# A gated memory over chunks: two steps of VectorE and ten of sixteen scatters change their place in the turn

## The reference, cut to what matters

```python
def step(carry, inp):                       # _L0_attn_ref, over 3137 tokens, 16 images
    M, n, m = carry
    qt, kt, vt, li, lf, op = inp
    m_next = jnp.maximum(lf + m, li)
    i_s = jnp.exp(li - m_next)
    f_s = jnp.exp(lf + m - m_next)
    M = f_s[:, :, None] * M + i_s[:, :, None] * (vt[:, :, None] * kt[:, None, :])
    n = f_s * n + i_s * kt
    h_raw = jnp.einsum('bij,bj->bi', M, qt)
    denom = jnp.maximum(jnp.abs(jnp.einsum('bi,bi->b', n, qt))[:, None], 1e-06)
    h = jax.nn.sigmoid(op) * (h_raw / denom)
    return ((M, n, m_next), h)
...
h = h + _L0_attn_ref(_layernorm(h, axis=-1), ...)        # rms norm of the output inside
h = h + _L0_ffn_ref(_layernorm(h, axis=-1), ...)
# _L0_ffn_ref: logits = x @ gate_w + gate_b; idx = argmax; pos = cumsum of the one-hot;
#              buf[idx, pos] = x; two layers by expert; gather back
```

## Time and profile before

| | us |
|---|---|
| median of 3 runs (3207.86 to 3208.52) | 3207.94 |
| the profiled execution | 3205.61 |
| its span from first to last instruction | 3203.7 |

### The profile page before, as it was taken

One profiled execution on the slowest core, in us unless ns is written; L12 is line 12 of the kernel. 1 busy time (PEld: TensorE's weight loads), 2 busy tenths in 40 slices (PEclk: granted clock), 3 DMA queues, 4 the chain that ended last, 5 costly groups with the idle time before them and its releaser, 6 DMA issues. The chain is left out here.

```text
span 3203.7 us, 68709 instructions
## 1 busy us (share of the span) xinstructions
PE 2828.8 (88%) x25818; PEld 1557.7 (49%) x25818; DVE 2414.1 (75%) x3224; ACT 2182.1 (68%) x3138; POOL 1916.0 (60%) x1191
## 2 busy tenths in 40 slices
PE   7999999969999999995599958899999999999997
PEld 5666666635555555553244413344444444444444
DVE  6888888858888888884387637777777777777783
ACT  6777777758887888872244447677777777777762
POOL 8888888811677777777200066666666666666530
PEclk9999999989999999996799969999999999999999
DMA  1111111111221221211444421111212211212111
GB/s 48 42 42 39 42 40 42 39 59 37 61 72 54 73 60 51 62 43 51 145 149 151 137 61 35 36 54 46 58 52 52 56 52 53 56 49 55 47 35 49
DMA packets 208269, 191.21 MB, mean 60 GB/s; under 512 B 76381, under 2 KB 163398, under 8 KB 207562
## 3 DMA queue, kind: packets, MB, share of 16 engines
q1 hardware_dynamic: 173850, 142.95, 15.4%
q0 software_dynamic: 25600, 26.01, 3.3%
q10 hardware_dynamic: 8496, 17.87, 1.5%
HBM read 99.08 MB, written 87.65 MB: 58 GB/s over the span
## 5 line engine op out<-in xcount | busy, mean ns | idle before, releaser
L2428 POOL TENSOR_TENSOR E_w<-E_w,E_rs 128x1024 f32<-128x1024 f32 x200 | 408.9, 2044 | 406.5 <-DVE E_rs L2336 406.5
L2421 POOL DMA_INDIRECT E_row<-yb,P_gi x400 | 388.4, 971 | 395.4 <-POOLq L93 301.6
L689 POOL DMA_INDIRECT xb<-B_yt,P_gi x400 | 469.0, 1172 | 115.4 <-issue 113.9
L204 POOL TENSOR_TENSOR A_kmask<-A_ksb,A_pack_a 128x3584 f32<-128x3584 f32 x56 | 356.2, 6361 | 115.3 <-ACT A_ksb L374 115.3
L2220 ACT ACTIVATE E_w<-E_w 128x1024 f32<-128x1024 f32 x200 | 211.6, 1058 | 241.0 <-DVE E_w L2329 241.0
L2333 DVE TENSOR_REDUCE E_sm<-E_w 128x16 f32<-128x1024 f32 x200 | 243.8, 1219 | 127.0 <-ACT E_w L2220 125.2
L2321 DVE TENSOR_REDUCE E_mx<-E_lg 128x16 f32<-128x1024 f32 x200 | 242.1, 1210 | 114.8 <-PE E_lg L1985 113.9
L474 DVE COPY A_vbd<-A_v 128x512 f32<-128x512 f32 x336 | 215.6, 684 | 74.3 <-PE A_v L324 74.3
L2329 DVE TENSOR_TENSOR E_w<-E_lg,E_mx 128x1024 f32<-128x1024 f32 x200 | 244.7, 1223 | 6.4
L2016 PEld LDWEIGHTS E_wt<-S_pack_f,E_w 128*128 128x128 f32 (+1 forms) x1600 | 169.6, 141 | 159.1 <-issue 132.6
L1985 PE MATMUL E_lg<-S_wxs,E_yo 64*128 64x512 f32 x800 | 228.0, 646 | 7.6 <-DVE E_w L2329 7.4
(11 more groups left out here) (321 smaller groups left out, 6803.3 us busy)
## 6 DMA issues: line engine op xcount, KB each, us to landing
R_xs<-xb SPq DMA_DIRECT2D x57, 256.0 KB, 2.7
yb<-R_ys SPq DMA_DIRECT2D x57, 256.0 KB, 2.0
B_x<-h SPq DMA_DIRECT2D x25, 512.0 KB, 4.0
h<-B_hh SPq DMA_DIRECT2D x25, 512.0 KB, 3.2
A_xg<-in_xw SPq DMA_DIRECT2D x56, 224.0 KB, 2.5
h<-A_res ACTq DMA_DIRECT2D x56, 224.0 KB, 2.5
E_hx<-h SPq DMA_DIRECT2D x48, 256.0 KB, 2.6
out<-E_ob SPq DMA_DIRECT2D x96, 128.0 KB
```

The lines of the kernel that those rows point to most:

```text
L204: nc.gpsimd.tensor_tensor(kmask[i % 2][:], bc(ksb[i % 2][:].unsqueeze(2), [128, J, H, Q]), bc(head_of_row[:].unsqueeze(1).unsqueeze(3), [1 ...
L689: pool.indirect_dma_start(out=xb, out_offset=bass.IndirectOffsetOnAxis(ap=routed.gi[0:k, c, b:b + 1], axis=0), in_=yt[c % LT][0:k, D * row ...
L2421: pool.indirect_dma_start(out=row[b % LR][:, k, i], out_offset=None, in_=yb, in_offset=bass.IndirectOffsetOnAxis(ap=idx[:, c, 2 * n + i:2 ...
L2428: TT(w3, w3, bc(rs[g % 3][:].unsqueeze(2), [128, 2 * SH, G]), ALU.mult).then_inc(w_done, 1)
```

## The change

No operation is added or taken away. On DVE `outputs` goes from the head of the turn (for chunk t-2) to the end of the turn before (chunk t-1), between `forget_middle` and `forget_sum`; `slots` and `numbers` go ahead of `norm_sum`; `norm_query` and `normed_out` go ahead of `forget_middle`. On POOL the first ten images of a chunk are scattered at the end of turn t = chunk + 4, and the other six in the turn after, between `weigh_keys` and `age_memory`; before, all sixteen went in turn chunk + 5, five of them at that place and eleven at the end.

```diff
                 for t in range(CHUNKS + 5):
                     at(weigh_keys, t - 1)
-                    at(scatter, t - 5, range(0, 5))
+                    at(scatter, t - 5, range(10, B))
                     at(age_memory, t - 2)
                     at(scale_memory, t - 1)
-                    at(scatter, t - 5, range(5, B))
+                    at(scatter, t - 4, range(0, 10))
...
                 for t in range(CHUNKS + 4):
-                    at(outputs, t - 2)
                     at(ends, t - 1)
                     at(exponents, t - 1)
                     at(first_max, t - 1)
...
                     at(ranked, t - 4)
                     at(first_norm, t - 1)
                     at(own, t - 4)
+                    at(slots, t - 4)
+                    at(numbers, t - 4)
                     at(norm_sum, t - 1)
-                    at(slots, t - 4)
                     at(gate_out, t - 1)
-                    at(numbers, t - 4)
                     at(norm_weight, t - 1)
+                    at(norm_query, t - 1)
+                    at(normed_out, t - 2)
                     at(forget_middle, t)
-                    at(norm_query, t - 1)
+                    at(outputs, t - 1)
                     at(forget_sum, t)
                     at(last_max, t - 1)
                     at(last_norm, t - 1)
-                    at(normed_out, t - 2)
```

## The result

The changed kernel takes 3271.45 us (median of 4 runs, 3263.53 to 3273.82), before 3207.9: 1.0188 times as long, 95% interval 1.0176 to 1.0201. The forecast of 3209 and its range to 3245 both missed. It went the way of rival D, and beyond D's 3244.

A forecast was written before the change was run, and what follows sets the result against it. PE and DVE's ring bound the turn, POOL second; after the change POOL sets it. First turns -1.4, twenty turns +12.4, end -12.7 and +3.0 give +1.3 us: 3209 us, range 3172 to 3245.

The forecast's parts named there:

- rival D: Second of POOL's ten scatters loses to `norm_weight`, B_kx falls behind `running_max`; turns 36 and 30, mean 33, 3244 us; chance 0.28.
- What bounds the kernel: Gated memory: PE alone needs 28.2 us a turn, the ring through B_yy 30.57; POOL second bound, 2.0 us free.
- Moves 1 and 2: DVE: earlier `normed_out` removes PE's 2.38 us wait; `outputs` ahead of `forget_sum` is covered by 3.35 us idle time.
- Move 3: DVE: `slots` and `numbers` before `norm_sum` make chosen rows ready at 20.95 instead of 24.1; about 0.55 us lost, covered.
- Move 4: POOL: sixth scatter ahead of `age_memory` costs `scale_memory` 0.73 us; B_mems becomes last to arrive at `turn_memory`.
- Six go free: POOL after `scale_memory`: first of ten scatters held 1.9 us by `norm_sum`, the next six not held.
- POOL never free: POOL has no idle time between turns 5 and 25; holds and waits 6.7 us, turn 31.3 us.
- A: The forecast chosen: turns of 31.3 us, 3209 us in all, own range 3200 to 3218; chance 0.36.
- First turns and end: POOL before B_kx of turn 5: -1.4 us; after the last B_kx ten scatters fewer, -12.7, and holds +3.0.
- Rival C: Only scatters are held, the two engines' arithmetic doesn't collide: turn 29.6 us, 3173 us; chance 0.10.

The follow-up runs named there:

- normed_only: The kernel before with `norm_query` and `normed_out` ahead of `forget_middle` and nothing else: 3219.63 us, ratio 1.0031.
- dve_moves_2: Repeat on a fourth chip of the kernel before with only the moves of `outputs`, `norm_query` and `normed_out`: 3200.25 us, ratio 0.9973.
- late_six: `dve_moves`, but POOL scatters six images a turn sooner, last in its turn, five ahead of `age_memory`, five after `scale_memory`: 3194.73 us, ratio 0.9953.
- the pairs: Three slow kernels against partners scattering chunk t-5 at the same places, old against fresh indices: turns 30.86 and 34.37, 30.82 and 33.74, 32.03 and 34.11 us.
- before_again: The kernel before, unchanged, run for its trace on a third chip: 3206.99 us (one run).
- dve_moves: The kernel before with only the moves of `outputs`, `norm_query` and `normed_out`: ratio 1.0358, on a chip where the kernel before took 3245.39 us.
- late_eight: `late_six` with eight instead of six scatters a turn sooner: 3199.94 us, ratio 0.9973.

## Why the prediction was wrong, point by point

- **What bounds the kernel**: right. With POOL's scatters nearly gone the turn is 28.15 (forecast 28.2 for PE alone), and POOL was the second bound.
- **Moves 1 and 2**: the wait of 2.38 us went, as said, but I booked `outputs` as a cost to be hidden. It is the half without which the wait only moves (`normed_only`). In `dve_moves_2` they bring 0.24 us a turn (30.68 to 30.43): POOL's holds grow by almost all that its waits shrink (busy 477.2 to 513.8).
- **Move 3, the indices**: the cast ended at 20.97 after `denominator`, forecast 20.95. What was mis-sized is the step behind it: I let the scatter start 0.1 us after the cast in each turn. It starts 0.95 after it in turn 4 and 0.8 in every later turn in which it waits. No row of before showed this passage, since there no scatter waited for its cast, and I gave it no bound. But it hardly mattered: the scatter falls inside `norm_sum` either way and is held to its end. Of the 0.87 that it starts late at most 0.2 reach the second scatter: scatters held in `norm_sum` without a wait end 0.78 after it, this one 0.97.
- **Move 4, "Six go free"**: this is the step that failed. By my own figures the second of the ten scatters (25.74) came behind the start of `norm_weight` (25.72), and by my own rule it was then to be held; I let it go free, and kept that case for rival D. Measured in turn 4: `norm_weight` starts 0.24 ahead of the second scatter, which takes 1.85 (0.88 held); the sixth and seventh are held 1.6, where one hold of 1.1 was forecast; and the tenth falls behind `running_max` (2.76, 1.79 held). The holds are 5.6 against 3.2, and B_kx is 40.0 us after `denominator`, forecast 36.65. How the row would have gone on with a free second scatter no run shows.
- **"POOL never free"**: wrong in kind. Its busy time rose by 37.7 us over twenty turns, 1.9 a turn; the other 31 us of the 68.7 are idle time. The schedule had no such waits; they come from the ring that fresh indices close: POOL waits for DVE's cast (27.4), is late with B_mems, PE starts its turn late, and POOL then waits for B_bw (46.8). Between the changed kernel and `late_six` these two waits, 74.2 against 0.3, are the whole difference of 73.5 us; the busy times are 514.9 and 514.1.
- **Rival D**: right in mechanism and in what tips it (the second scatter behind `norm_weight`, B_kx late), and alternately 36 and 30 forecast, where PE's turns were 38.4 and 29.8. It was not right in all its order: it had `running_max` hold B_kx, but the tenth scatter was held; it had `age_memory` held by `norm_sum`, but `age_memory` just got in and `scale_memory` was held. B_mems ends 26.8 after `denominator`, D's "near 27". And from B_kx to B_kx, where it expected 30 and 36, came 33.1 and 35.2. The term it lacked is PE's clock after the idle time: 2.75 us in each long turn (11.59 instead of 8.84 from `turn_memory` on), 1.4 a turn on the mean, 28 over twenty. With it D's mean of 33 would have been 34.4, measured 34.11, and its 3244 would have been 3272; without it even D was short. The trace of before could have warned me. In two of its twenty turns `denominator` was slow behind a wait of 2.4 us, at a granted clock of 0.84 over the next 9 us, and the turn 1.5 us longer:

```profile
967.30 3.42 PE L711 MATMUL B_PD<-B_nq,B_pack_b 128*128 128x512 f32 x4 [2.38 <-DVE B_yy L1213]
```

  I gave D 0.28 and chose A, whose margins I had myself found to be 0.02 to 0.1 us: with such margins the cases should have been nearly equal, and the range should have reached beyond D.
- **First turns and end**: forecast -1.4 and -9.7, measured +4.1 and -6.5. Of the first, 1.9 us is there at the stage's first `denominator` (729.96, 728.06 before), and nearly all of that already at PE's first matmul of L711 (691.2, before 689.4), ahead of all that the change touches. That start moves from execution to execution (689.3 to 691.9 over the traces of the kernels here), so these 1.9 are not the change's. The rest of the miss, 3.35, is turn 4's lateness (40.0 for 36.65).
- **Rival C and the page**: the Trainium skill ("SBUF — State Buffer", section "Who interferes with whom") infers that descriptor generation on GpSimd is not blocked by a two-input step of DVE; by that the prediction had turns of 28.2. The rows of 2.33, 1.85 and 2.76 speak against it, as the earlier trace rows did. The lock between the two engines' arithmetic, which it also states, is seen in B_mems (2.96 for 1.04) and B_cm (4.51 for 2.30).

## What to carry to other kernels

Before work is pulled a turn ahead, ask for each of its inputs in which turn it is made: to use an input in the turn that makes it can close a ring between two engines, and if what follows on the waiting engine feeds a third (here B_mems for PE), each loses what the other was waiting. Put such work last in the waiting engine's turn, behind work with old inputs; in `late_six` that, with one scatter fewer ahead of `age_memory` and the indices at their old place, turned 1.019 into 0.995, and 2.1 of the 3.7 us a turn are the fresh indices by the pairs. Count a wait of TensorE at more than its length where a trace shows that such waits cost it its clock: here 2.5 us did in 39 turns of 65. When an early step is to remove a wait, look at the waiting engine's next instruction too: if its input stands later in the same list, both must move. And where a schedule worked out has margins below a tenth of a microsecond, it is no forecast between its cases.

## What the hardware showed that I had not expected

- From the end of a 128x16 cast on DVE to the start of the indirect DMA that waits for it: 0.8 us, 0.95 the first time in each kernel, while scatters that wait for nothing start 0.3 apart.
- The cast itself, ordinarily 0.17 us, took up to 1.42 beside a POOL multiplication.
- After 5.8 us idle PE ran four 128x512 matmuls in 3.78 us instead of 1.98. In the twenty turns of each of fifteen traces (all but `before_again` and those of the chip of `dve_moves`), PE's work from `turn_memory` on took 1.3 us or more beyond 8.84 each time after a wait of over 4.6 us there (30 of 30), 39 times of 65 after one of 2.5, and never after one of 1.2 (132).
- On the chip of `dve_moves` the kernel before took 37 us more than on the other five, and in that run PE's matmuls came four or five at a time with 1 us between; the same kernel was faster than before on another chip. What differs on that chip stays open.
- Scatters that began inside a DVE step with two SBUF inputs were held until 0.77 to 1.03 us past its end, also where they began almost with it; only some that began within 0.03 us of its start took their plain 0.97.
- POOL's extra 1 us ahead of a scatter every five turns in `late_eight`: not explained.
